# Gated cross-attention with a routed feed-forward on one core: the last iterations rearranged, and the third batch's k projection and turning of x put into the first wait

## The reference, cut to what matters

```python
x = x + tanh(g_xattn) * attention(layernorm(x), ctx, ctx)      # 16 batches, 256 tokens, E = 256, 16 heads of 16
h = layernorm(x)
scores = softmax(h @ w_router)                                 # 8 experts
weights, experts = top_k(scores, 2)
expert(e) = (silu(h @ w1[e]) * (h @ w3[e])) @ w2[e]            # hidden size 512
x = x + tanh(g_ffn) * (shared(h) / 3 + (2/3) * sum over the two experts of weight * expert(h))
```

## Time and profile before

| | |
|---|---|
| median of three runs | 824.37 us (824.17 to 826.52) |
| profiled execution, its own time | 821.54 us |
| its span, first to last instruction | 819.8 us |
| TensorE's mean granted clock | 0.994 of 2.4 GHz |
| PE busy | 771.5 us (94%) |
| DVE busy | 543.3 us (66%) |
| ACT busy | 413.4 us (50%) |
| POOL busy | 432.0 us (53%) |
| DMA | 127.34 MB, 154 GB/s over the span |

### The profile page before, as it was taken

How to read it: one execution, slowest core, us unless ns; L and a number is a source line. 1 busy time by engine, 2 the same in 40 slices (tenths; PEclk the granted TensorE clock), 3 DMA queues, 4 the chain that set the end, 5 groups by cost and what they waited for, 6 DMA issues and landing times.

```text
span 819.8 us, 19446 instructions
## 1 busy us (share of the span) xinstructions
PE 771.5 (94%) x6977; PEld 688.4 (84%) x6978; DVE 543.3 (66%) x1118; ACT 413.4 (50%) x690; POOL 432.0 (53%) x486
## 2 busy tenths in 40 slices
PE   4889999999999999988998999999999999999997
PEld 4766777777777766568998999999999999999996
DVE  5677789998888898946564444444444444456787
ACT  5767776777777776742334324343333343333331
POOL 5633446666666655466571566656757584236000
PEclk9999999999999999999999999999999999999999
DMA  6855556766666653253487343324333422218522
GB/s 205 275 179 164 187 182 229 227 225 216 211 213 208 206 175 124 96 183 130 146 231 265 75 128 85 113 68 119 99 106 82 121 53 75 54 57 327 219 81 74
DMA packets 129102, 127.34 MB, mean 155 GB/s; under 512 B 55184, under 2 KB 110992, under 8 KB 129040
## 3 DMA queue, kind: packets, MB, share of 16 engines
q1 hardware_dynamic: 114896, 80.34, 32.8%
q0 software_dynamic: 14144, 46.19, 16.1%
HBM read 75.32 MB, written 50.91 MB: 154 GB/s over the span
## 4 chain that ended last, share of the span: by engine, by line
PE 51%; POOL 14%; DMA 13%; issue 9%; DVE 7%; ACT 4%; SPq 2%; POOLq 1%; ACTq 0%; DVEq 0%
PE bank L561 6%; POOL w_l L1610 6%; PE bank_ss L613 5%; PE bank L563 5%; PE bank L562 5%; DMA y_d<-y_s,y_rows 5%; PE bank L642 5%; DMA y_rows<-xs_d 4%; PE bank_sm L626 4%; PE bank_sm L561 3%; PE bank_sm L562 2%; PE bank_sm L563 2%; PE bank_ss L561 2%; PE bank L649 2%; PE bank_ss L563 2%
## 5 line engine op out<-in xcount | busy, mean ns | idle before, releaser
L1247 DVE TENSOR_REDUCE row_max<-bank_sm 128x4 f32<-128x1024 f32 x124 | 151.5, 1222 | 38.2 <-PE bank_sm L626 36.8
L952 ACT ACTIVATE probs_T<-bank_ss 128x1024 f32<-128x1024 f32 x123 | 126.4, 1027 | 18.8 <-PE bank_ss L613 18.5
L1226 DVE TENSOR_TENSOR gT_l<-gg,gT_h 128x1024 fp32r<-128x1024 f32 x49 | 66.7, 1360 | 103.1 <-ACT gT_h L1083 103.1
L561 PE MATMUL bank_sm<-xg_h,w_h 128*128 128x256 f32 x400 | 115.1, 288 | 4.5 <-DVE xg_l L1226 4.4
L561 PE MATMUL bank<-w_h,gT_h 128*128 128x256 f32 x392 | 111.4, 284 | 3.2 <-DVE gT_l L1226 3.2
L562 PE MATMUL bank_sm<-xg_h,w_l 128*128 128x256 f32 x400 | 114.4, 286 | 0.0
L563 PE MATMUL bank_sm<-xg_l,w_h 128*128 128x256 f32 x400 | 114.3, 286 | 0.0
L561 PE MATMUL bank_ss<-xg_h,w_h 128*128 128x256 f32 x400 | 113.2, 283 | 0.0
L562 PE MATMUL bank_ss<-xg_h,w_l 128*128 128x256 f32 x400 | 112.9, 282 | 0.0
L563 PE MATMUL bank_ss<-xg_l,w_h 128*128 128x256 f32 x400 | 112.9, 282 | 0.0
L562 PE MATMUL bank<-w_h,gT_l 128*128 128x256 f32 x392 | 110.9, 283 | 0.0
(11 more groups left out here) (203 smaller groups left out, 1951.7 us busy)
## 6 DMA issues: line engine op xcount, KB each, us to landing
qk_d<-qk_s SPq DMA_DIRECT2D x64, 256.0 KB, 3.0
w_raw<-wall POOLq DMA_DIRECT2D x27, 512.0 KB, 3.9
k<-qk_d SPq DMA_DIRECT2D x48, 256.0 KB, 4.1
q<-qk_d SPq DMA_DIRECT2D x48, 256.0 KB, 4.6
xq<-xs_d SPq DMA_DIRECT2D x140, 64.0 KB, 2.2
y_pairs<-y_d POOLq DMA_DIRECT2D x16, 512.0 KB, 8.8
x<-x SPq DMA_DIRECT2D x16, 256.0 KB, 4.7
c_s<-ctxT SPq DMA_DIRECT2D x16, 256.0 KB, 3.0
```

Of the source, the lines that this page charges most:

```text
L561: pe.matmul(out, ah, bh, start=first and k == 0, stop=False)
L952: act.activation(pT[:, 2 * (pv % 4):2 * (pv % 4) + 2, :].rearrange("p h t -> p (h t)"), exp_bank(V.b, pv)[:, :], ACT.Exp, scale=D ** -0.5) ...
L1226: return v.tensor_tensor(dst, ps, high.bitcast(F32), ALU.subtract)
L1247: v.tensor_reduce(mx[B.slot][:, :, :].rearrange("p t (r q) -> p r t q", r=2)[:, :, :, p], max_bank(B.b, p)[:, :].rearrange("p (r t k) -> p ...
```

## The change

1. First wait, PE: of iteration -1's 28 idle matmuls of 256 columns, seven of 512 columns are left, and between them stand the k projection (`project_k`) and the turning of x (`turn_x`) of batch 2, which stood at p = 1 and p = 2. Two other groups of 8 idle matmuls become 4 of 512 columns. On DVE the statistics of batch 3 (`stats_ahead`, `variance_ahead`) go ahead of the first row maximum.
2. Turn between the stages: logits of x13 and x14 go to another place (`lg_tail`, in bank T2), and PE's waits for `lgc_ok` behind them go, but for one ahead of `down(0)`. ACT's `head_out(x15, 3)` goes ahead of `silu(0)`. PE's `turn_norm(x15)` goes behind `up1(2)`, logits, rank and count of x15 go later by a step. DVE's `x_low_shared(2, 2)` and `(3, 3)` go ahead of `list_slots`. POOL's two roots go ahead of the cuts.
3. Routed tiles: `turn_rows` writes to PSUM bank 4 in place of `xrT`, which is gone; the first one goes ahead of `gated(5)`.
4. The load of 4 MB becomes four of 1 MB, each behind the tiles of one of the first four experts.
5. The end: the two weighted pairs of batches 14 and 15 are added in four of the last tiles' steps (`PAIR_AT`), between `gated` and `g_low`; `mix(14)` and the four operations ahead of the last output go, and one operation gives batch 14's output.

```diff
+X2_PARTS = 4
...
-                    pe.matmul(at, wt_h[:, 1, 0, 0:P], wt_h[:, 1, 0, :], start=True, stop=True)
+                    pe.matmul(at, wt_h[:, 1, 0, 0:P], wt_h[:, 1, :, :].rearrange("p c n -> p (c n)"), start=True, stop=True)
...
                     if B and among_first(B, 1) and p == 0:
-                        keep_warm(SS[:, 0:L], 28)
+                        keep_warm(SS[:, 0:512], 2)
+                        project_k()
+                        keep_warm(SS[:, 0:512], 3)
+                        turn_x()
+                        keep_warm(SS[:, 0:512], 2)
...
-            logits(x13)
-            pe.wait_ge(lgc_ok, x13.n(1, 1))
+            logits(x13, lg_tail)
             project_out(x14)
...
-            logits(x14)
-            pe.wait_ge(lgc_ok, x14.n(1, 1))
+            logits(x14, lg_tail)
             project_out(x15)
             rank(x14, rk_tail)
             up3(1, SHARED)
             pe.wait_ge(vr_ok, NB)
             pe.wait_ge(pos_ok, NB - 3)
+            pe.wait_ge(lgc_ok, x14.n(1, 1))
             down(0, SHARED)
+            up1(2, SHARED)
             turn_norm(x15)
-            up1(2, SHARED)
-            logits(x15)
             up3(2, SHARED)
+            logits(x15, lg_p)
+            down(1, SHARED)
             rank(x15, rk_tail)
-            down(1, SHARED)
...
             probs(x15, PAIRS - 1)
+            head_out(x15, 3)
             silu(0)
-            head_out(x15, 3)
...
                 def before(p):
 
+                    if p == 0 and Eb and Eb.b == R:
+                        stats_ahead()
+                        variance_ahead()
...
-                v.transpose(xrT[:, :, :].rearrange("p c (t q) -> p c t q", q=QD),
+                v.transpose(psX[:, :].rearrange("p (c t q) -> p c t q", c=EC, q=QD),
                             xq[:, :, :].rearrange("p t (c j) -> p c t j", c=EC)).then_inc(xt_ok, 1)
...
+            PAIR_AT = {NB - 5: (NB - 1, 0), NB - 4: (NB - 1, 1), NB - 3: (NB - 2, 0), NB - 2: (NB - 2, 1)}
...
                     gated(end + (j - EARLY))
+                    if j in PAIR_AT:
+                        add_pair(*PAIR_AT[j])
                     g_low(end + (j - EARLY))
...
             po.wait_ge(oh_ok, x14.n(1, 1))
+            root(bmv2, rstd2, var2_ok, x15, rstd2_ok)
             cut(1, 0, which=(1,))
-            root(bmv2, rstd2, var2_ok, x15, rstd2_ok)
...
-            po.wait_ge(x2_st, NB * 16)
-            po.dma_start(x2a[:, :, :], x2_d.rearrange("b p d -> p b d")).then_inc(x2_in, 16)
...
+                if e < X2_PARTS:
+                    n = NB // X2_PARTS
+                    po.wait_ge(x2_st, NB * 16)
+                    po.dma_start(x2a[:, e * n:(e + 1) * n, :], x2_d[e * n:(e + 1) * n].rearrange("b p d -> p b d")).then_inc(x2_in, 16)
```

More of the change, by code:

```diff
@@ L719, in one, with project_k, turn_x @@
                 A, B, C, S, S2, S3 = (stage(i, k) for k in (3, 1, 0, -1, -2, -3))
+                def project_k():
+                    pe.wait_ge(cl_ok, A.n(1, 1))
+                    if among_first(A, R):
+                        moved(pe, kh_ok, A.n())
+                    else:
+                        pe.wait_ge(vr_ok, A.n())
+                    weights(A, 1)
+                    for oc in range(EC):
+                        project(T2, 1, oc, c_h[A.c_slot], c_l[A.c_slot], k_ps)
+                def turn_x():
+                    pe.wait_ge(xn_ok, A.n(1, 1))
+                    if C:
+                        pe.wait_ge(mT_ok, C.n(1, 1))
+                    if S2:
+                        pe.wait_ge(oTl_ok, S2.n(1, 1))
+                    else:
+                        moved(pe, xnTl_ok, A.n())
+                    if A.b == 0:
+                        pe.wait_ge(k_in, 16)
+                    if A.b == 2:
+                        pe.wait_ge(gbo_ok, 1)
+                    transposes(T0, xn_s, xnT_ps)
                 for p in range(PAIRS):
@@ L735, in one @@
                     if p == 1 and S3:
[L736 to L745, removed]
+                        logits(S3, lg_p)
+                    if p == 1 and A and A.b != R - 1:
+                        project_k()
                     if p == 2 and S:
                         values(S, 3)
[L748 to L760, removed]
+                    if p == 2 and A and A.b != R - 1:
+                        turn_x()
                     if p == 3 and A and among_first(A, R):
@@ L1447, in _ @@
             gated(0)
-            best_two(x14)
+            best_two(x14, lg_tail)
             masks(x14)
@@ L1459, in _ @@
             g_low(1)
-            best_two(x15)
+            best_two(x15, lg_p)
             masks(x15)
+            x_low_shared(3, 3)
+            gated(2)
             positions(x15, rk_tail)
             list_slots(x15)
-            x_low_shared(3, 3)
-            gated(2)
+            g_low(2)
             v.wait_ge(cnt_ps, 1)
@@ L1506, in _ @@
             g_low(4)
+            v.wait_ge(pos_ok, NB)
+            turn_rows(EARLY)
             gated(5)
@@ L1708, in _ @@
             po.wait_ge(mx_ok, NB * PAIRS)
+            root(bmv2, rstd2, var2_ok, x14, rstd2_ok)
             cut(1, 0, which=(0,))
-            root(bmv2, rstd2, var2_ok, x14, rstd2_ok)
             scatter(x13, 0)
```

78 lines of the change are left out of this document (45 added, 33 removed).

## The result

The changed kernel took 819.75 us (median of 8 runs, 815.51 to 823.56) against 825.25 of the kernel before beside it: ratio 0.9934, 95% interval 0.9907 to 0.9961. It is faster by some 5.5 us. 16.5 were forecast, and 819.75 lies above the range of 803 to 815. Two later comparisons gave 818.82 against 824.96 (0.9921, 0.9893 to 0.9949) and 815.90 against 825.55 (0.9901, 0.9861 to 0.9940). (The ratios are those on record. They need not be the quotients of the two medians.)

The account below looks back on a forecast made before the run. PE was taken as the bound, busy 771.5 of 819.8 us, with gains only at its stops, slow stretches and the end. Terms summed to -16.55 us: 805.0 profiled, given as a median of 807.9, range 803 to 815.

Parts of the forecast that it names:

- First wait (-1.0): PE's first wait: new work fits, first scores unmoved; DVE statistics moved ahead bring everything behind the last maximum 1.0 us earlier.
- Logits (-1.5): Turn between stages: with their own place for the logits, PE skips two waits of 0.75 us for their reader.
- `head_out` (-1.45): Turn between stages: PE's stop for `oT` goes once ACT's `head_out(x15, 3)` runs ahead of `silu(0)`, 1.45 us.
- `turn_norm(x14)` (-0.6): Turn: root ahead of a POOL cut shortens PE's 1.56 us stop by 0.6; norm beside the cut may add 0.3.
- the turn gives back only part: Rival, 0.17: vector operations and cuts slow each other, both `turn_norm` still wait, the clock still falls; +4.4, 812.3 us.
- `turn_norm(x15)` (-3.8): Turn: 24 `up1(2)` matmuls ahead of the transposes cover PE's 2.37 us stop; its slow stretch, 1.4, goes too.
- What they lead to, lists and the first load of a routed tile, has slack: Turn: x15's logits, rank and count may move a step later; load issued at 401.57, tile needed at 422.20.
- The load in four parts: Routed tiles: splitting the 4 MB load removes the third tile's 2.35 us stop and its 1.4 us slow stretch, -3.7.
- the parts on POOL (+0.2): Expert changes: four issues of 0.8 us, against faster cuts with rows in PSUM and a shorter `gT_l` wait; together +0.2.
- POOL becomes the bound: Rival, 0.17: at expert changes each part costs POOL 1.5 us with nothing given back; +5.8, 813.7 us.
- PSUM: Routed tiles: turned rows in PSUM end the slow `xg_l` beside a cut, none over 0.8 us; counted within +0.2.
- The end (-2.9): Kernel's end: with pair operations moved earlier, the last output needs PE alone and ends at 814.6, not 817.49.

Follow-up runs that it names:

- the statistics alone: The base with PE's order of before in the first wait, DVE's statistics and variance still ahead of the first maximum: 808.52 us, 0.9832.
- the base: The changed kernel with the second routed tile's rows in their own buffer, loaded ahead of the clears, and the four load parts in the last two experts: 808.79 us, 0.9823.
- the base with part 1 undone: The base with k projection, turning of x and statistics where they stood before, and 14 idle matmuls in the first wait: 809.37 us, 0.9840.
- part 1 alone: The kernel before with only the first-wait edit (part 1) of the change: 822.46 us, 1.0001.

## Why the prediction was wrong

The kernel is faster, as forecast, and by one third of the amount. Several steps held on their own. The largest failure is in the sum, which let a gain ahead of a chain of DMAs pass through it. Besides, terms were sized from single stops of one execution that the two further profiles with the old order of the turn do not all repeat.

- **First wait (-1.0): failed.** "They fit, so the first scores start no earlier or later" holds (30.13 against 30.35), and DVE's maxima were 0.86 us shorter where the statistics alone went ahead. The failing words are that the k projection taken out of PE's work between the scores could only gain (the end at -1.5). Without it there the clock fell in eleven of twelve profiles. Alone the part is worth nothing: 1.0001 (0.9979 to 1.0023).
- **Logits (-1.5) and `head_out` (-1.45): right.** None of these stops is in any profile of the changed kernel.
- **`turn_norm(x14)` (-0.6): wrong, it costs time.** In the first profiles the stop fell from 1.56 to 0.74 us, but over the fourteen profiles with the new order it is 0.38 to 2.39 us, 1.17 in the mean, against 1.56, 0.54 and none with the old one (the last with 0.64 for `xg_l` behind it). Behind it stands in each of the fourteen a new stop of 1.01 or 1.02 us for `xg_l` of a shared tile, and in five of them the granted clock of a stretch between 366 and 372 us is 0.50 to 0.56. The step that failed is the price of "the norm behind it now runs on DVE while POOL cuts", at most 0.3 us in the prediction. DVE's norm before, and its norm and `xg_l` in the changed kernel, beside POOL's cut there:

```profile
366.20 0.74 DVE L1313 TENSOR_SCALAR xn<-x_s,bn_mv,rstd 128x256 f32<-128x256 f32 x2 [1.77 <-POOL rstd L1628]
```

```profile
363.15 2.46 DVE L1324 TENSOR_SCALAR xn<-x_s,bn_mv,rstd 128x256 f32<-128x256 f32 x2
365.52 1.75 DVE L1237 TENSOR_TENSOR xg_l<-xsT,xg_h 128x512 fp32r<-128x512 f32 x1
```

```profile
364.18 2.55 POOL L1645 TENSOR_TENSOR w_l<-w_raw,w_h 128x512 fp32r<-128x512 f32 x2
```

  The root indeed came in time, and DVE's wait of 1.77 us for it is gone, but DVE now needs 1.7 us more for the norm and 1.0 more for `xg_l` (0.71 before). These are the lengths in all fourteen profiles (2.38 to 2.46 and 1.68 to 1.75) against 0.74 and 0.69 to 0.71 in the three others. The rival "the turn gives back only part" had named this mechanism.
- **`turn_norm(x15)` (-3.8): the stop right, the clock a draw.** 2.37 us became 0 to 0.47, the half clock behind it is gone, and 0.54 us at `gg` is new. But of the three profiles with the old order (2.37, 2.37 and 1.07 us) only the first has that half clock, 1.4 us of the term. With the first routed tile (-1.8, right) the stretch gave 6.0 of 8.4 us.
- **"What they lead to, lists and the first load of a routed tile, has slack": this sentence failed, and it cost the most.** It looked at the first load only. From the turning of the second tile's rows to PE's start on it pass 2.14 us (430.52 to 432.66). In the kernel before they were turned at 425.10 and PE came at 430.91, so the slack was 3.7 us, less than the 6 by which PE came earlier, and the first tile's early turn sent their load into the middle of seven clears. The difference of 6 and 3.7 accounts for the stop of 2.1 to 2.3 us that stands even where the rows landed early; the late landing makes it 6 to 7. Together that cost 4.4 us on average, and 7.1 came back when the load was put ahead of the clears. The prediction had no term for this, nor a rival.
- **The load in parts (-3.7) and the parts on POOL (+0.2): mis-sized together.** The stop at the fourth tile (my "third") is gone, but with the whole load it is no more than 0.90 us either, since PE comes late. And 2.35 us with 1.4 of half clock behind it was itself the largest of three draws: the others are 0.35 and 1.61 us, both without half clock. On POOL the issue took 0.80 us as counted; at one change it drew 1.14 us more with it and moved ACT's copy: 2.8 to 3.3 us of stop and half clock. With the parts elsewhere 3.4 us came back. The rival "POOL becomes the bound" named the place and the mechanism (5.8 us in all); it came true at one change of expert of the four.
- **PSUM: right.** No `xg_l` of a routed tile over 0.7 us, as forecast, and some 2 us fewer waits of PE. (That of a shared tile, whose inputs stayed in SBUF, is the one of 1.75 us above.)
- **The end (-2.9): exact.** The last rows of the changed kernel:

```profile
814.64 0.28 PE L564 MATMUL bank_sm<-w_l,w_h 128*128 128x256 f32 x1
```

```profile
814.96 0.48 DVE L1623 SCALAR_TENSOR_TENSOR oo<-bank_sm,gate_scaled,x_all 128x256 f32<-128x256 f32 x1 [0.17 <-PE bank_sm L564]
```

DVE ends 0.52 us behind PE in all three profiles, 3.43 before. The pair operations show no cost where they went: at 776.68 one pair stands between `gg` and `gT_l`, and the idle time ahead of `gT_l` is 0.62 us in place of 1.13.

With the two largest causes mended the kernel comes near the forecast of 807.9 us: 808.79 with part 1 as it is, 808.52 with PE's old order in the first wait, ratios 0.9823 (0.9789 to 0.9856) and 0.9832 (0.9794 to 0.9870). Both beat the kernel before and the changed one. The nearness is in part luck: beside 822.66 us, the kernel before on that chip, 808.79 is a gain of 13.9 us where 16.5 were forecast, and the terms of the first wait and of `turn_norm(x14)` are still missing in it.

## What to carry to other kernels

When a change lets an engine arrive earlier, follow every transfer that it will then want earlier, not only the next one, and compare each one's slack with the whole gain: here the second tile's 3.7 us met a gain of 6. A load that a faster step sends out early may fall among others and land later, as in three of five executions here; put it ahead of them, if need be with a buffer more. Before moving one engine's work out of another's way, look at what will then run beside it: the root came early enough, and the cut behind it made DVE's norm three times as long. Size a term from more than one profile. And work that stands between the pieces of another engine's chain may be what keeps the clock: before moving it, look at what is left in its place.

## What the runs showed of the hardware

- One kernel, two landing times: the second tile's rows came 12.6 or 16.3 to 16.9 us behind POOL's last clear, with the load's issue 0.13 us behind that clear in the one case and 0.07 and 0.33 us ahead of it in the other; whether the order or the chip decides is open. PE's stop was 2.13 us in the one case and 6.12 and 6.96 in the other. It may be part of why this kernel's runs spread from 813.9 to 823.6.
- A load of 1 MB took 6.5 us from issue to landing (median of four), the one of 4 MB 17.4, so the times of four add up to 26 us in place of 17.4. I had taken a quarter, 4.35. The Trainium skill ("DMA: Bandwidth & Descriptors", section "Anatomy of one DMA") points that way with its fixed part of about 2 us for each.
- DVE and POOL slowed each other where both worked: DVE's two norm operations took 0.74 us together with no cut beside them and 2.38 to 2.46 us beside one, the subtraction `xg_l` with both inputs in SBUF 0.69 to 0.71 and 1.68 to 1.75 us. In the routed tiles the same subtraction with one input in PSUM took 694 ns at most over 34 tiles (the base), and up to 1820 ns with both in SBUF again.
- The clock also fell between 50 and 54 us in some executions and not in others of the same kernel (0.57 and 0.68 in the first two profiles of the changed kernel, 0.50 in the third; 1.00 in both of before). It was 0.50 in the base with part 1 undone, so the new order of the first wait is not needed for it, and 0.57 with part 1 alone. Which part of the change, if any, brings that on is open.
